# Cross-attention kernel on one core: query and key stacking moved from VectorE to GpSimd and ScalarE, exponentials ahead of the rounding

## What is computed

```python
Q = (decoder_input @ W_q).reshape(B, Sd, HEADS, HEAD_DIM)      # 16 heads of 8
K = (encoder_output @ W_k).reshape(B, Se, HEADS, HEAD_DIM)
V = (encoder_output @ W_v).reshape(B, Se, HEADS, HEAD_DIM)
scores = jnp.einsum('bqhd,bkhd->bhqk', Q, K) / jnp.sqrt(jnp.float32(HEAD_DIM))
attn = jax.nn.softmax(scores, axis=-1)
out = jnp.einsum('bhqk,bkhd->bqhd', attn, V).reshape(B, Sd, E)
return out @ W_o + b_o
```

## Time and profile before

| | |
|---|---|
| median of 3 runs | 213.25 us (212.55 to 214.83) |
| the profiled execution's own time | 213.41 us |
| its span (first to last instruction) | 211.6 us |
| mean granted TensorE clock | 0.969 |

### The profile page before, as it was taken

How to read it: one execution, slowest core, us unless ns; L and a number is a source line. 1 busy time by engine, 2 the same in 40 slices (tenths; PEclk the granted TensorE clock), 3 DMA queues, 4 the chain that set the end, 5 groups by cost and what they waited for, 6 DMA issues and landing times.

```text
span 211.6 us, 4097 instructions
## 1 busy us (share of the span) xinstructions
PE 181.0 (86%) x1300; PEld 139.4 (66%) x1300; DVE 154.5 (73%) x437; ACT 116.8 (55%) x229; POOL 58.5 (28%) x85
## 2 busy tenths in 40 slices
PE   5699799899999999999999678789999999888231
PEld 4389498678799888889899355546555666445110
DVE  2889758667468565654767996799899999965684
ACT  2257467742322222443354289977989797858242
POOL 3714274691000000300220164333223232304400
PEclk9999999999999999999999999999999999999755
DMA  6999300000000000000000000000000000000002
GB/s 221 378 417 377 137 0 2 0 3 0 0 0 5 0 0 3 0 0 0 3 0 0 2 0 5 0 5 0 2 3 0 0 0 0 0 3 0 0 2 99
DMA packets 4225, 8.81 MB, mean 42 GB/s; under 512 B 880, under 2 KB 1904, under 8 KB 3952
## 3 DMA queue, kind: packets, MB, share of 16 engines
q1 hardware_dynamic: 2480, 7.60, 9.3%
q10 hardware_dynamic: 1728, 1.00, 1.6%
HBM read 5.98 MB, written 0.52 MB: 31 GB/s over the span
## 4 chain that ended last, share of the span: by engine, by line
PE 58%; DVE 19%; issue 9%; ACT 8%; POOL 2%; DMA 2%; DVEq 1%; ACTq 0%; POOLq 0%
PE banks L1176 12%; PE bank L1010 7%; PE bank L1012 7%; PE bank L1011 7%; DVE negm L860 6%; PE bank L1207 5%; PE bank L1241 4%; ACT rest L468 2%; PE banks L1012 2%; PE banks L1011 2%; PE banks L1010 2%; DVE stats L610 2%; PE bank L1250 2%; ACT raw L493 2%; DMA xs<-in_x 2%
## 5 line engine op out<-in xcount | busy, mean ns | idle before, releaser
L860 DVE TENSOR_REDUCE negm<-bank 128x2 f32<-128x512 f32 x64 | 42.0, 687 | 2.4 <-PE bank L1207 1.5
L435 ACT ACTIVATE att<-bank 128x512 f32<-128x512 f32 x32 | 19.2, 599 | 38.4 <-PE bank L1012 25.7
L300 POOL TENSOR_TENSOR keyed<-rest,const 32x256 fp32r<-32x256 f32 x32 | 19.5, 608 | 61.2 <-DVE rest L850 49.9
L493 ACT ACTIVATE raw<-banks 128x1024 f32<-128x1024 f32 x32 | 32.5, 1023 | 3.5 <-PE banks L1226 3.2
L1207 PE MATMUL bank<-keyed 128*128 128x512 f32 x64 | 25.9, 447 | 4.1 <-DVE negm L860 1.8
L815 DVE SCALAR_TENSOR_TENSOR xs<-banks,rw,xs 128x128 f32<-128x128 f32 x64 | 18.0, 344 | 5.9 <-PE banks L1176 5.8
L1176 PEld LDWEIGHTS banks<-raw,attT 128*128 128x128 f32 x176 | 21.3, 192 | 0.8
L1176 PE MATMUL banks<-raw,attT 128*128 128x128 f32 x176 | 21.4, 275 | 0.0
L1010 PE MATMUL bank<-xT,w 128*128 128x512 f32 x48 | 19.9, 416 | 1.4 <-DVE xT L744 1.4
L1207 PEld LDWEIGHTS bank<-keyed 128*128 128x128 f32 x64 | 10.7, 188 | 12.7 <-issue 9.4
L1011 PE MATMUL bank<-xT,w 128*128 128x512 f32 x48 | 18.8, 391 | 0.0
(11 more groups left out here) (201 smaller groups left out, 390.2 us busy)
## 6 DMA issues: line engine op xcount, KB each, us to landing
raw<-in_w SPq DMA_DIRECT2D x1, 2048.0 KB, 10.7
keyed<-negm SPq DMA_DIRECT2D x1, 2048.0 KB, 8.8
raw<-in_w SPq DMA_DIRECT2D x1, 1024.0 KB, 9.8
xs<-in_x SPq DMA_DIRECT2D x2, 256.0 KB, 3.4
ctxT<-in_ctxT SPq DMA_DIRECT2D x1, 512.0 KB, 4.6
ctx<-in_ctx SPq DMA_DIRECT2D x1, 512.0 KB, 6.5
wl<-in_wl SPq DMA_DIRECT2D x1, 256.0 KB, 6.8
wqkraw<-in_wq ACTq DMA_DIRECT2D x1, 256.0 KB, 7.1
```

What stands on the lines that cost most here:

```text
L300: pool.tensor_tensor(km[rows, g, j, :], ks[rows, g % 2, :], const[rows, C_ZERO:C_ZERO + 1].broadcast_to([QUAD, SEQ]), ALU.add)\
L435: act.activation(silus[:, k, :], bk[2 * k][:, :], ACT.Silu).then_inc(S["silu_s"], 1)
L493: act.activation(probs[:, slot, 2 * r:2 * r + 2, :, :].rearrange("p h k q -> p (h k q)"), pair[r][:, :], ACT.Exp, scale=ATT_SCALE).then_in ...
L860: dve.tensor_reduce(negm[:, g % 2, r // 2, c0:c0 + QUAD + 1:QUAD], bk[1 + r % 2][:, :].rearrange("p (h k) -> p h k", h=2), AX.X, ALU.max, ...
```

## The change

GpSimd makes the query stack (`queries`) and adds the keys' two parts straight into all four quadrants of `km`. The masks move to ScalarE's rounding, as a scale per partition, and ScalarE copies the whole projection to SBUF (`rwb`), since GpSimd reads it there. VectorE stacks nothing any more. On ScalarE both exponentials of a group come before the rounding. The turned maxima alternate between banks 1 and 2, score piece 0 comes after the whole projection, the outputs are multiplied in two halves, the normalising of the earlier batch moves, the bias additions move from groups 1 and 3 to 4 and 6, and all 16 groups are written out without a loop. `heads_out` has five slots in place of four.

```diff
+        qraw, kraw = rwb[:, 0:2, 0:SEQ], rwb[:, 0:2, SEQ:2 * SEQ]
+        hiK = w14[:, :, :].rearrange("p b d -> p (b d)").rearrange("p (u k) -> p u k", u=2)
...
-            def masked_keys(m, g, first):
-                pool.wait_ge(S["ks_s"], m + 1)
-                if not first:
-                    pool.wait_ge(S["s2_ps"], 2 * (m - 3))
-                for j in range(2, HPG):
+            def queries(m):
+                pool.wait_ge(S["q_hi"], m + 1)
+                pool.wait_ge(S["qk_raw"], m + 1)
+                if m >= G:
+                    pool.wait_ge(S["s1_ps"], 4 * (m - 3))
+                    pool.wait_ge(S["qa_s"], m - 3)
+                pool.tensor_tensor(qs[:, m % G, :], qraw[:, m % 2, :], hiQ, ALU.add).then_inc(S["qs_s"], 1)
+                pool.wait_ge(S["qs_s"], m + 1)
+
+            def masked_keys(m):
+                pool.wait_ge(S["k_hi"], m + 1)
+                pool.wait_ge(S["qk_raw"], m + 1)
+                if m >= G:
+                    pool.wait_ge(S["s2_ps"], 2 * (m - G + 1))
+                for j in range(HPG):
                     rows = slice(QUAD * j, QUAD * (j + 1))
-                    pool.tensor_tensor(km[rows, g, j, :], ks[rows, g % 2, :],
-                                       const[rows, C_ZERO:C_ZERO + 1].broadcast_to([QUAD, SEQ]), ALU.add)\
-                        .then_inc(S["km_pool"], 1)
-                    pool.wait_ge(S["km_pool"], 2 * m + j - 1)
+                    pool.tensor_tensor(km[rows, m % G, j, :], kraw[rows, m % 2, :], hiK[rows, m % 2, :], ALU.add)\
+                        .then_inc(S["km_s"], 1)
+                    pool.wait_ge(S["km_s"], HPG * m + j + 1)
...
+            for m in range(GROUPS):
+                b, g = m // G, m % G
+                if g == 1 and b > 0:
+                    values(b, False)
+                if m + 2 < GROUPS:
+                    queries(m + 2)
+                    masked_keys(m + 2)
+                if m == 0:
+                    deviation_and_shift(1)
+                if m in (G, G + 2):
+                    add_bias((m - G) // 2)
...
             def proj_hi(m, bank=0):
                 act.wait_ge(S["proj_ps"], m + 1)
-                queries_hi(m, bank)
-                keys_hi(m, bank)
+                act.wait_ge(S["qs_s"], m)
+                act.activation(hiQ.bitcast(r32), bk[bank][:, 0:SEQ], ACT.Copy, scale=const[:, C_AQ:C_AQ + 1])\
+                    .then_inc(S["q_hi"], 1)
+                if m >= 2:
+                    act.wait_ge(S["km_s"], HPG * (m - 1))
+                act.activation(hiK[:, m % 2, :].bitcast(r32), bk[bank][:, SEQ:2 * SEQ], ACT.Identity,
+                               scale=const[:, C_AK:C_AK + 1], bias=const[:, C_ONE:C_ONE + 1]).then_inc(S["k_hi"], 1)
+                act.copy(rwb[:, m % 2, :], bk[bank][:, :]).then_inc(S["qk_raw"], 1)
...
+            def act_group(m):
+                b, g = m // G, m % G
+                if 2 <= m < GROUPS - 1:
+                    o_copy(m - 2)
+                exps(m, 0)
+                if m in (2, 3):
+                    later_norm_hi(g)
+                if m in TURNED_AT:
+                    turned_out(b - 1)
+                exps(m, 1)
+                if m + 3 < GROUPS:
+                    proj_hi(m + 3)
...
-                    if ahead:
-                        stack_queries(m + 2, (g + 2) % G, first and g < 2)
-                        stack_keys(m + 2, (g + 2) % G, first and g < 2)
...
+            def dve_group(m):
+                b, g = m // G, m % G
+                more = m + 1 < GROUPS
+                if more:
+                    maxima(m + 1, 0)
+                shifted(m)
+                if more:
+                    maxima(m + 1, 1)
+                if more:
+                    maxima(m + 1, 2)
+                if m == 0:
+                    sum_moments(1)
+                if m in (2, 3):
+                    later_norm_lo(g)
+                if g == 0 and b >= 2:
+                    add_attention(b - 2, slice(TPB * (b - 2), TPB * (b - 1)))
+                if b > 0 and g == 1:
+                    normalise(b - 1, 0)
+                if 0 < b < BATCH - 1 and g == 2:
+                    normalise(b - 1, 1)
+                if more:
+                    maxima(m + 1, 3)
...
+            def scores(m, r):
+                t, half = r // 2, r % 2
                 pe.wait_ge(S["qs_s"], m + 1)
+                pe.wait_ge(S["km_s"], HPG * m + 2 * (half + 1))
...
+                turn_maxima(m)
+                bank7_free(m)
+                if m >= 2:
+                    outputs(m - 2, LOW, 0 if final else 7)
+                if more:
+                    scores(m + 1, 1)
+                if m >= 2 and not final:
+                    outputs(m - 2, HIGH)
+                if more:
+                    scores(m + 1, 2)
+                shifted_scores(m)
...
+                if more:
+                    scores(m + 1, 3)
...
+                if m + 3 < GROUPS:
+                    project(m + 3)
+                if m + 2 < GROUPS:
+                    scores(m + 2, 0)
```

More of the change, by code:

```diff
@@ L311, in add_bias @@
                 pool.wait_ge(S["bo_added"], h + 1)
[L313 to L322, removed]
             pool.wait_ge(S["ctx_lo"], 1)
@@ L471, in proj_hi @@
             def proj_hi(m, bank=0):
                 act.wait_ge(S["proj_ps"], m + 1)
-                queries_hi(m, bank)
-                keys_hi(m, bank)
-            def masked_keys(m, g, first):
-                act.wait_ge(S["ks_s"], m + 1)
-                if not first:
-                    act.wait_ge(S["s2_ps"], 2 * (m - 3))
-                for j in range(2):
-                    rows = slice(QUAD * j, QUAD * (j + 1))
-                    ins = act.copy(km[rows, g, j, :], ks[rows, g % 2, :])
-                ins.then_inc(S["km_act"], 1)
@@ L545, in _ @@
             proj_hi(2)
-            act_batch(0, True, False)
-            with act.Fori(1, BATCH - 1) as b:
-                act_batch(b, False, False)
-            act_batch(BATCH - 1, False, True)
+            for m in range(GROUPS):
+                act_group(m)
             def chunk_norm(c):
@@ L862, in maxima, with shifted @@
                                       AX.X, ALU.max, negate=True).then_inc(S["s1_max"], 1)
-            def shifted(m, g, first):
+            def shifted(m):
                 dve.wait_ge(S["mT_ps"], m + 1)
                 dve.wait_ge(S["qs_s"], m + 1)
-                if not first:
+                if m >= G:
                     dve.wait_ge(S["s2_ps"], 2 * (m - 3))
-                dve.tensor_tensor(qa[:, g, :], bk[2][:, 0:SEQ], plain(qs[:, g, :]), ALU.add).then_inc(S["qa_s"], 1)
+                dve.tensor_tensor(qa[:, m % G, :], bk[1 + m % 2][:, 0:SEQ], plain(qs[:, m % G, :]), ALU.add)\
+                    .then_inc(S["qa_s"], 1)
@@ L938, in _ @@
             dve.wait_ge(S["setup"], 1)
-            maxima(0, 0, range(2), True)
+            maxima(0, 0, 1)
             weigh(UNITS - 1)
-            maxima(0, 0, range(2, 4), True)
-            dve_batch(0, True, False)
-            with dve.Fori(1, BATCH - 1) as b:
-                dve_batch(b, False, False)
-            dve_batch(BATCH - 1, False, True)
+            maxima(0, 2, 3)
+            for m in range(GROUPS):
+                dve_group(m)
             def chunk_out(c):
@@ L1196, in scores, with project @@
[L1196 to L1208 removed]
+            def project(m, bank=0):
+                pe.wait_ge(S["qk_raw"], m)
+                b, g = m // G, m % G
+                cols = slice(b * SEQ, (b + 1) * SEQ)
+                for a, src in enumerate((xT, ctxTs)):
+                    ins = three(bk[bank][:, a * SEQ:(a + 1) * SEQ],
+                                (wqk[:, 0, a, g * P:(g + 1) * P], wqk[:, 1, a, g * P:(g + 1) * P]),
+                                (src[:, 0, cols], src[:, 1, cols]), True, True)
+                ins.then_inc(S["proj_ps"], 1)
@@ L1220, in shifted_scores @@
                 pe.wait_ge(S["qa_s"], m + 1)
+                g = m % G
                 for t in range(TPB):
                     for j in range(HPG):
-                        if not first and t == 0 and j % 2 == 0:
+                        if m > 0 and t == 0 and j % 2 == 0:
                             pe.wait_ge(S["p_s"], 2 * (m - 1) + j // 2 + 1)
@@ L1338, in _ @@
                 if n >= UNITS - 2:
[L1339 to L1340 removed]
+                    project(n - UNITS + 2, 7)
                 up(n)
```

320 lines of the change are left out of this document (113 added, 207 removed).

## The result

The change makes the kernel slower: 226.8 us (226.37 to 227.87) against 213.8 us of the kernel before timed beside it, a ratio of 1.062 with a 95% interval of 1.055 to 1.069. The forecast was 211.0, and the measured time lies far above its range. The profiled execution has a span of 225.2 us where the old one had 211.6.

What follows compares the result with a forecast made beforehand. VectorE, over 90% busy, bounded the old kernel; ScalarE to GpSimd was to bind the new. Gains of 1.4 and 1.5 less losses of 0.2 and 0.3 gave 2.4: span 209.2, plus 1.8, 211.0 us; range 207.6 to 214.4.

Steps and rivals of the forecast that it cites:

- S: TensorE's second score matmul of the next group, needing all four key parts; claimed to start 0.88 us after the turn.
- the turn: Start of the span where a group turns its maxima (L1215); the first, at 119.09, was claimed to stay.
- 0.22 + 0.51 + 0.22: On TensorE, from S to the start of the shifted scores, 0.95 us in all.
- ScalarE to GpSimd becomes the loop: TensorE was to wait for GpSimd's keys, made after ScalarE's work: S to S two groups on, at least 8.37 us.
- The term of GpSimd: GpSimd's five two-operand additions, 0.61 us each (bounds 0.40 and 0.95); all four key parts ready after 3.34.
- The steps of VectorE and TensorE: Their loop over the maxima, per group: plain 3.54 us, with transposed outputs normalised 4.50, with the output layer 4.30.
- the plain step: One group of the VectorE and TensorE loop without normalising or output layer, 3.54 us.
- VectorE's relief: VectorE loses its two stackings a group, 13.4 us together, while the kernel was to gain about 2.4.
- ScalarE's three operations: On ScalarE after the exponentials: queries' part 0.47 us, keys' part 0.57, copy of 512 columns 0.58.
- the loop over the values' copy: In groups 5, 9 and 13 GpSimd refreshes the values before the keys: S to the next S takes 4.92 us.
- A: Rival: GpSimd's path is shorter, VectorE and TensorE stay the bound; gain 5.6, 207.8 us; chance 0.20.
- C: Rival: GpSimd's additions each grow by 0.17, about seven crossings, 6.0 added: 217.0 us, kernel slower; chance 0.12.

Runs made afterwards that it cites:

- e1_whole: The changed kernel with the outputs of a group's four heads undivided, as before the change; 214.56 us, ratio 1.003 to the kernel before.
- e2: The kernel before with only the outputs divided: two heads, one score matmul, two heads; 225.74 us, ratio 1.057.
- e11: The changed kernel with query stack on VectorE and its normalising and adding behind the last maximum, outputs divided by heads; 222.71 us, ratio 1.042.
- e8: The changed kernel with undivided outputs, a broadcast column of zeros as second operand of GpSimd's five additions; 212.57 us, ratio 0.995.

## Why the prediction was wrong

**The step that failed** is "S starts 0.37 + 0.51 = 0.88 after the turn (L1215 to L1241, then half of 1.02)", and behind it the 0.51 in "0.22 + 0.51 + 0.22". It took half the heads for half the time. The runs showed 0.99 for each half, and 0.43 for each of the two score matmuls in place of 0.22. So from the turn to the shifted scores the prediction has 0.88 + 0.95 = 1.83 us, the kernel after 3.21 (168.15 to 171.36), and the undivided one 2.06 (166.56 to 168.62). By this group the division costs TensorE 1.15 us of work, some 15 us in 13 groups; between the first and the last turn its busy time is 74.8 us against 60.7 in e1_whole, 14.1 more. Of that 2.0 go into idle time that TensorE had (9.7 us in e1_whole, 7.7 here), and the stretch is 12.2 longer; e1, e2 and e11 measured 12.5, 12.1 and 12.0 for the whole kernel. The reason was in the code: each head has a `tile_position` in a column quadrant of its own. And the number was in the trace of before, in the last group, where this kernel already divides its outputs; TensorE there:

```profile
188.86 1.06 PE L1241 MATMUL bank<-raw,vones 128*32 128x256 f32 x8
...
190.29 1.06 PE L1241 MATMUL bank<-raw,vones 128*32 128x256 f32 x8
```

Eight records take 0.99 us, where sixteen took 1.02. No duration had to be guessed: this row has the very form of the new code.

With it fell the path. The forecast had "ScalarE to GpSimd becomes the loop", and no term for TensorE's own work, though TensorE was busy for 17.27 of 17.99 us in batch 2, more than VectorE, and had 0.2 us of idle time in a group to take anything more. In the kernel after it is busy for 21.75 of 22.84. Its score matmuls did not wait for GpSimd in most groups: the trace has such idle time as at 174.06 in 4 places, 3.0 us in all.

**The term of GpSimd** was mis-sized: 0.61 expected, 0.73 measured, 3.94 from the start to the last key part in place of 3.34. The nearest rows taken, L254 and L300, have one broadcast column as second operand (L254 an `rinv` per partition, not the two full operands that the prediction names), and e8 shows that this is the difference. GpSimd did work on two full operands in the kernel before, in subtractions elsewhere in the span:

```profile
L260 POOL TENSOR_TENSOR w<-raw,w 128x512 fp32r<-128x512 f32 x8 | 10.1, 1284 | 6.6 <-ACT w L368 5.2 <-issue 1.4
L277 POOL TENSOR_TENSOR wqk<-wqkraw,wqk 128x1024 fp32r<-128x1024 f32 x1 | 2.4, 2406 | 0.0
```

1.284 us for 512 columns and 2.406 for 1024 are 0.561 for each 256, and 1.284 - 0.561 gives an estimate of 0.72 for 256 columns: the measured value, from rows of the kernel before. The bounds, 0.40 and 0.95, held it. In the changed kernel it can show only in the 4 places where TensorE waits for keys; in the undivided form it is worth 1.6 us.

**The steps of VectorE and TensorE** (3.54, 4.50, 4.30) were too short even for the undivided form. They rested on a score matmul that comes in the middle of the outputs, 0.88 after the turn. In e1_whole the step of group 11, without a normalising, is 4.24 and that of group 10, with one, 4.96 (turns at 166.56, 171.52 and 175.76). Score piece 1 comes 1.39 after the turn (166.56 to 167.95), and VectorE idles 0.80 before its maximum. These 0.51 are most of the 0.70 by which the plain step was short.

**What was right.** VectorE's relief is not worth its size; the first turn and the tail stayed (119.50 for 119.09, 23.12 for 23.08); ScalarE's three operations take 0.48, 0.58 and 0.61 for 0.47, 0.57 and 0.58; the loop over the values' copy holds its group (from S at 169.51 the values' copy starts 1.64 later for 1.0, since the second output half lies between, and the keys take 3.94 for 3.34; with the 0.48 of the copy and the 0.10 of the handover that makes 6.16 from S to S, 169.51 to 175.67, for 4.92). Two of its own signs of being wrong came: additions above 0.7, and a stretch of groups 8 to 11 over 19 us. One slip in its numbers changes nothing: the lower end, "A's value, 207.6", is 207.8 by A's own sum.

**The rivals.** C gave 217.0 for slower additions; it named the right sign and the wrong place. The additions did not grow beside VectorE's work, and 0.12 each is worth 1.6 us in the undivided kernel, where C's working (five additions, seven crossings) makes 4.2 of them. For GpSimd's addition against VectorE's stacking, 0.73 against 0.475 is 1.5. That lies between the prediction's 1.3 and the factor of two that it cites from the Trainium skill, "GPSIMD Engine Reference", section 4.1, and nearer to the 1.3. None of the rivals had TensorE's own work growing, because a division of work into pieces was priced at nothing.

**Left open.** No run isolates why a score matmul takes 0.43 beside the outputs and 0.22 ahead of another. Of the rest of the change, which loses 0.3% together in e1_whole, only the query stack's engine, the second operand, ScalarE's order and the place of VectorE's normalising and adding were tried one by one; the banks of the turned maxima, the place of score piece 0, the bias additions and the loop written out were not.

## What to carry to other kernels

A division of work into pieces is an edit with a price of its own, even when the matmuls stay the same in number: ask which units work side by side in the whole, and whether they still do in a piece. Here half the heads took as long as all, and a division by keys, which keeps all four quadrants at work, cost a third of it (4.3 of 12.5 us, part of them a wait for GpSimd). Before an edit is priced, ask also how much idle time the engine that gets the work has. Look first for a row of the kernel before that already has the form of the new code, here the last group's two halves, and for a nearest row with operands of the same kind, not only of the same size.

## What the runs showed of the hardware

- Matmuls of 128x32 weights over 256 fp32 columns, on two column quadrants: 8 records in 0.99 us; on four: 16 records in 1.02 us, 8 in 0.57.
- A 512-column score matmul between two such pieces takes 0.43 us to the next start, against 0.22 when another of its kind comes right behind it.
- GpSimd's addition over 256 columns takes 0.61 us with one column broadcast as second operand (e8) and 0.73 with two full operands (the kernel after), whether on 32 or 128 partitions.
